# Alternating search depth, and a first search ahead of the projection, in a two-layer graph network kernel

## What is computed

```python
h = relu(layernorm(x))                      # layer 0
src_rows = h[src]                           # 200000 x 32: the gather
msg = sum over 9 coefficients of coef[e,c] * (src_rows @ W0[c])
x = x + segment_sum(msg, dst)

h = relu(layernorm(x))                      # layer 1
msg = sum over 16 bases of wcomp[type[e],b] * (h[src] @ W1[b])
a = tanh(relu(sum((h[src] @ A1.T + b1) * (h[dst] @ A2.T + b2 + rel[type])) / sqrt(32)))
x = x + relu(segment_sum(a * msg, dst) + h[src[last edge]] @ W_self)
```

## Time and profile before

| | us |
|---|---|
| median of 3 runs | 3520.62 (3517.32 to 3525.52) |
| the profiled execution | 3504.08 |
| its span, first to last instruction | 3502.3 |
| PE busy | 3104.4 (89%) |
| DVE busy | 2749.0 (78%) |
| POOL busy | 2353.0 (67%) |
| ACT busy | 883.5 (25%) |

### The profile page before, as it was taken

One profiled execution on the slowest core, in us unless ns is written; L12 is line 12 of the kernel. 1 busy time (PEld: TensorE's weight loads), 2 busy tenths in 40 slices (PEclk: granted clock), 3 DMA queues, 4 the chain that ended last, 5 costly groups with the idle time before them and its releaser, 6 DMA issues. The chain is left out here.

```text
span 3502.3 us, 110849 instructions
## 1 busy us (share of the span) xinstructions
PE 3104.4 (89%) x42844; PEld 2581.4 (74%) x42844; DVE 2749.0 (78%) x4092; ACT 883.5 (25%) x1910; POOL 2353.0 (67%) x2481
## 2 busy tenths in 40 slices
PE   3999999999999999999978888888888888888887
PEld 2777777777777777777767777777777777777776
DVE  7777777777777777777768888888888888888886
ACT  1001001001001001001034443334444444444443
POOL 5666666666666666666537777777777777777772
PEclk9999999999999999999969999999999999999998
DMA  4111111111111111111123333333333333333331
GB/s 130 26 23 25 25 23 25 25 23 25 25 23 25 25 23 25 25 23 25 23 67 57 54 55 56 56 56 56 55 57 57 57 56 56 57 57 56 56 57 39
DMA packets 218214, 149.97 MB, mean 43 GB/s; under 512 B 121914, under 2 KB 199003, under 8 KB 217821
## 3 DMA queue, kind: packets, MB, share of 16 engines
q0 software_dynamic: 79232, 40.73, 11.8%
q1 hardware_dynamic: 138013, 100.79, 11.7%
q10 hardware_dynamic: 576, 2.40, 0.2%
HBM read 135.47 MB, written 8.22 MB: 41 GB/s over the span
## 5 line engine op out<-in xcount | busy, mean ns | idle before, releaser
L538 POOL DMA_INDIRECT xg<-h_table,idx x2476 | 2342.1, 946 | 1091.5 <-issue 721.3
L606 PE MATMUL ps<-h,blocks 128*128 128x448 f32 x9100 | 1921.0, 369 | 23.1 <-DVE blocks L947 23.1
L606 PEld LDWEIGHTS ps<-h,blocks 128*128 128x128 f32 x9100 | 1692.7, 188 | 229.4 <-issue 78.4
L947 DVE TENSOR_TENSOR blocks<-scratch,ps 128x896 fp32r<-128x896 int16 x650 | 703.0, 1082 | 117.1 <-PE ps L606 113.1
L1038 DVE TENSOR_TENSOR Z<-coef,ps 128x864 f32<-128x864 f32 (+1 forms) x522 | 734.3, 1448 | 16.6 <-DVE ps L979 0.2
L672 PE MATMUL ps<-Z,xg 128*32 128x32 f32 (+3 forms) x25008 | 505.9, 215 | 4.9 <-DVE Z L1038 4.9
L826 ACT ACTIVATE p_left<-ps 96x128 f32<-96x128 f32 (+2 forms) x262 | 64.3, 245 | 1734.9 <-PE ps L642 1617.6
L1056 DVE TENSOR_TENSOR aggT<-aggT,ps 64x128 f32 (+1 forms) x262 | 74.1, 283 | 515.0 <-PE ps L654 515.0
L672 PEld LDWEIGHTS ps<-Z,xg 128*32 128x32 f32 x25008 | 403.8, 110 | 88.8 <-issue 67.6
L956 DVE SCALAR_TENSOR_TENSOR scratch<-ramp_sb,scratch,ps 128x448 f32<-128x448 f32 x650 | 438.3, 674 | 0.2
L961 DVE TENSOR_REDUCE xg<-scratch 128x32 f32<-128x448 f32 x650 | 402.7, 620 | 22.3
(11 more groups left out here) (105 smaller groups left out, 1048.7 us busy)
## 6 DMA issues: line engine op xcount, KB each, us to landing
xg<-h_table,idx POOLq DMA_INDIRECT x2476, 2.4
rows_b<-typ_short SPq DMA_DIRECT2D x130, 258.0 KB
scratch<-q_short SPq DMA_DIRECT2D x260, 96.0 KB, 3.3
rows_b<-dst_short SPq DMA_DIRECT2D x130, 126.0 KB
coef<-in_edge_dram SPq DMA_DIRECT2D x130, 54.0 KB, 1.9
att_tab<-p_table SPq DMA_DIRECT2D x393, 8.1 KB
p_table<-Z SPq DMA_DIRECT2D x8, 297.0 KB, 3.8
X<-in_x_dram SPq DMA_DIRECT2D x7, 224.0 KB, 5.0
```

The lines of the kernel that those rows point to most:

```text
L538: pool.indirect_dma_start(xg[:, g.q, t - g.s * J, :], None, h_table[n], bass.IndirectOffsetOnAxis(ap=idx[:, t:t + 1], axis=0)).then_inc(L. ...
L606: last = pe.matmul(found_ps[b], blocks[:, b, c, :], h_2[:, a, c], start=(c == 0 and a == 0), stop=(c == NCH - 1 and a == 1))
L947: dve.tensor_tensor(blocks[:, b], q_b[:, g.b, NPM - NP[n] + i, :].unsqueeze(1).broadcast_to([P, NCH, P]), block_ps.unsqueeze(2).broadcast_ ...
```

## The change

Three things. (1) In layer 0 the number of searched tiles depends on the group: 3 in even groups, 2 in odd ones, where it was 3 in all. POOL gathers the other 9 or 10. Layer 1 keeps 2. (2) In PE's step the search of the group's first tile stands ahead of the projection; the other searches stay behind it. (3) In DVE's step the first mask stands ahead of the addition; `found_rows` makes the addition between the first mask and the first pick. The remaining lines are the counting that goes with it: semaphore values now come from `tiles_before`, buffer parities from the sum of the tiles before, and the loads of the mask numbers always bring three tiles' worth, as before.

```diff
-NP = [3, 2]
-NPM = max(NP)
+NP = [[3, 2, 3, 2], [2, 2, 2, 2]]
+NPM = max(max(np) for np in NP)
...
+    def tiles_before(self, n, later=0):
+
+        r = self.r + later
+        of_pass = FULL // 4 * sum(NP[n]) + sum(NP[n][0:FULL % 4])
+        return self.k * of_pass + (self.i + r // 4) * sum(NP[n]) + sum(NP[n][0:r % 4])
...
-        return [(i, J - NP[n] + i, (self.b * NP[n] + i) % 2, (self.full_order() - 1) * NP[n] + i + 1) for i in range(NP[n])]
+        np = NP[n][self.q]
+        return [(NPM - np + i, J - np + i, (sum(NP[n][0:self.q]) + i) % 2, self.tiles_before(n) + i + 1) for i in range(np)]
...
-                    wait(sp, L.block_set, (g.full_order() - 2) * NP[n])
+                    wait(sp, L.block_set, g.tiles_before(n, -1))
...
                 def step(gs):
+                    tiles = gs[0].found_tiles(n) if gs[0] else []
+                    find_rows(tiles[0:1])
                     if gs[2]:
                         project(gs[2])
-                    if gs[0]:
-                        find_rows(gs[0])
+                    find_rows(tiles[1:])
...
-                def found_rows(new, old):
-
-                    old_tiles = old.found_tiles(n) if old else []
+                def found_rows(new, old, back):
+
+                    old_tiles = old.found_tiles(n)[-2:] if old else []
                     new_tiles = new.found_tiles(n) if new else []
-                    for i in range(max(len(old_tiles), len(new_tiles))):
-                        if new_tiles:
+                    for i in range(max(len(old_tiles), len(new_tiles), 1)):
+                        if i < len(new_tiles):
                             block_rows(new, new_tiles[i])
-                        if i < 2 and old_tiles:
-                            pick_rows(old, old_tiles[i - 2 if NP[n] > 1 else 0])
-                        if i >= 2 and new_tiles:
+                        if i == 0 and back:
+                            add(back)
+                        if i < len(old_tiles):
+                            pick_rows(old, old_tiles[i])
+                        if 2 <= i < len(new_tiles):
                             pick_rows(new, new_tiles[i - 2])
...
                 def step(gs):
-                    if gs[3]:
-                        add(gs[3])
-                    found_rows(gs[0], gs[1])
+                    found_rows(gs[0], gs[1], gs[3])
```

More of the change, by code:

```diff
@@ L86 @@
 assert NOWHERE < 1 << 15 and NREL <= 1 << 8
-assert NCH * MC == M and FULL % 2 == 0 and JT <= JH and PS <= P
+assert NCH * MC == M and FULL % 2 == 0 and all(sum(np) % 2 == 0 for np in NP) and JT <= JH and PS <= P
 def gathers_of_pass(n, q):
-    return len(range(q, FULL, 4)) * (J - NP[n]) + (JT if q == FULL % 4 else 0)
+    return len(range(q, FULL, 4)) * (J - NP[n][q]) + (JT if q == FULL % 4 else 0)
 class Group:
@@ L120, in halves @@
         return -(-self.nj // JH), min(self.nj, JH) * WN
-    def full_order(self):
-        return self.k * FULL + self.s + 1
     def full_order2(self):
@@ L133, in gathers @@
             return gathers_of_pass(n, self.q)
-        return (self.i + self.r // 4 + 1) * (J - NP[n])
+        return (self.i + self.r // 4 + 1) * (J - NP[n][self.q])
     def gathered_tiles(self, n):
-        return self.nj if self.tail else J - NP[n]
+        return self.nj if self.tail else J - NP[n][self.q]
+    def tiles_before(self, n, later=0):
+        r = self.r + later
+        of_pass = FULL // 4 * sum(NP[n]) + sum(NP[n][0:FULL % 4])
+        return self.k * of_pass + (self.i + r // 4) * sum(NP[n]) + sum(NP[n][0:r % 4])
     def found_tiles(self, n):
@@ L597, in edge_sums, with find_rows @@
                 weights = w0c if n == 0 else w1_sb
-                def find_rows(g):
-                    for i, j, b, o in g.found_tiles(n):
+                def find_rows(tiles):
+                    for i, j, b, o in tiles:
                         pe.wait_ge(L.block_set, o)
@@ L663, in sum_edges @@
                     if not g.tail:
-                        pe.wait_ge(L.picked, g.full_order() * NP[n])
+                        pe.wait_ge(L.picked, g.tiles_before(n, 1))
                     pe.wait_ge(L.Z_set, g.order() * 2 - 1)
@@ L946, in block_rows @@
                     wait(dve, L.found, o - 2)
-                    dve.tensor_tensor(blocks[:, b], q_b[:, g.b, NPM - NP[n] + i, :].unsqueeze(1).broadcast_to([P, NCH, P]),
+                    dve.tensor_tensor(blocks[:, b], q_b[:, g.b, i, :].unsqueeze(1).broadcast_to([P, NCH, P]),
                                       block_ps.unsqueeze(2).broadcast_to([P, NCH, P]), ALU.is_equal).then_inc(L.block_set, 1)
@@ L952, in pick_rows @@
                     i, j, b, o = tile
-                    u = g.s * NPM + NPM - NP[n] + i
+                    u = g.s * NPM + i
                     dve.wait_ge(L.found, o)
@@ L1003, in scores @@
                     if not g.tail:
-                        dve.wait_ge(L.picked, g.full_order() * NP[n])
+                        dve.wait_ge(L.picked, g.tiles_before(n, 1))
                     dve.wait_ge(L.ex_done, o)
```

## The result

| | before | the change |
|---|---|---|
| median of 4 runs, us | 3521.82 (3517.32 to 3525.52) | 3295.32 (3294.23 to 3295.84) |
| ratio, 95% interval | 1 | 0.9357 (0.9341 to 0.9373) |
| profiled execution, its span | 3504.08, 3502.3 | 3295.84, 3294.0 |
| last gather, last addition of layer 0 | 1739.95, 1779.99 | 1580.04, 1607.47 |
| first gather, last gather, last addition of layer 1 | 1803.56, 3444.12, 3483.36 | 1630.86, 3258.61, 3275.05 |

The forecast was 3296 us. The time is met, but by luck: two misses cancel in it. From profile to profile the change saves 208.2 us, not 223.6: layer 0 gave 172.5 us where 187.9 were expected, and layer 1, from its first gather to its last addition, 35.6 where 35.7 were.

A forecast was written before the change was run, and what follows sets the result against it. PE was taken to bound layer 0 and POOL layer 1, with POOL next in layer 0; 187.9 + 35.7 = 223.6 us off 3504.1 gives 3280.5, times 1.0047 is 3296 us, range 3283 to 3345.

The forecast's parts named there:

- Depth in layer 0 (189 us of PE): Layer 0: 65 odd groups lose one search of 2.90 us each, 189 us less for PE.
- A gain of about 0.2 us a group, 26 us in all: Layer 0: with the first search ahead of the projection, PE waits about 0.65 us a group instead of 0.85.
- So POOL is the next bound: Layer 0: two groups need 23.7 us of POOL, 22.9 of PE; the layer ends 187.9 us sooner.
- The wait of PE for rows ahead of the sums: Sign expected in layer 0: besides its wait ahead of the first search, PE has another ahead of the sums.
- rival A: PE stays the bound because its new wait exceeds 0.65 us: 150 us gained in all, 3370 us; chance 0.17.
- up to 0.85 us POOL still decides: Layer 0: with PE's new wait up to 0.85 us, POOL, not PE, would still be the bound.
- Layer 1: PE's round falls to 11.8 us, POOL at 12.48 us a group is the bound: 35.7 us less.
- The 0.47%: Whole kernel: the runs' median lay 0.47% above the profiled execution; carried over, 3280.5 us becomes 3296.
- The rule on the shared port: VectorE in a 2-port mode locks GpSimd out; no such instruction is added, so gathers stay at 944 ns.
- B: Layer 1 gains nothing, as DVE becomes its bound through exposed register load and scatter: 3333 us; chance 0.05.
- C: TensorE's clock falls as PE waits for rows before the sums: about 4160 us at a third of both layers; chance 0.03.
- D: The first search is not ahead at all, its pick coming too late: 3335 us as a median; chance 0.05.

The follow-up runs named there:

- e1: Only the alternating depth in layer 0, old order in both layers, against the kernel before on another chip (4876.75 us): costs 2.2%.
- e6: The alternating depth alone in the old order, run again on a further chip where the kernel before takes 4940.36 us; its total is not given, shortest two-search round 10.26 us.
- e4: The kernel before without an edit, profiled on another chip: its one execution took 4869 us, 7 us under the median of the other seven.

## Why the prediction was right, and where it was not

- **Depth in layer 0 (189 us of PE).** Right in kind: 65 searches went to POOL, and a round with two searches is 13.11 - 10.26 = 2.85 us shorter than one with three, where 2.90 were taken as a third of a stretch (the 10.26 is from undisturbed rounds of e1 and e6). 65 x 2.85 is 185 us, more than the whole gain of layer 0.
- **"A gain of about 0.2 us a group, 26 us in all".** This step failed. The wait was 0.77 us, not 0.65: from the end of the pick's multiplication to the search it is 1038.12 - 1037.98 = 0.14 us, not 0.06, and in the even group of the rows shown the pick starts 0.36 us behind the addition, not 0.23. And the border that the projection now makes between searches costs about 0.16 us (8.87 against 8.71, 6.03 against 5.87), which the forecast's value took as nothing and only its upper bound as 0.3. So 0.08 us of waiting was saved and 0.16 spent. Instead of 12.9 and 10.0 us PE needs 13.25 and 10.33. The order costs 0.07 us in an odd group and 0.14 in an even one, 65 x 0.07 + 66 x 0.14 = 14 us in layer 0: 185 - 14 leaves 171, measured 172.5. That the order costs this much is worked out from rounds, those of the depth alone on other chips; no run on the first chip has the depth alone.
- **"So POOL is the next bound".** This fails with it. PE needs 13.25 + 10.33 = 23.58 us per two groups, not 22.9, and POOL's 23.72 is longer by only 0.14. POOL does run without a pause, and its dates were met (fifth group 81.98, forecast 80.7; last gather 1580.04, forecast 1579.6), but its lead was used up only by 12.6 us, the difference of the two tails, instead of 27.5. The wait of PE for rows ahead of the sums, which the forecast named as a sign, isn't there (0.0 us at L675). The layer ended when PE was done, 15.4 us later than forecast. That is rival A in a mild form: the forecast held PE's slack for 27 us, and it was 15 us below zero. By the forecast's own rule, "up to 0.85 us POOL still decides", a wait of 0.77 was harmless; the rule left out the border.
- **Layer 1.** Right, 35.6 against 35.7 us. From first to last gather POOL took 1627.8 us instead of 1640.6, and last gather to last addition shrank by 22.8. The search does start earlier than the projection did: PE waits 102.6 / 113 = 0.91 us where it waited 1.47. But the round fell only from 12.58 to 12.27 us, not to 11.8: here too the searches, 5.78 us in one stretch, take 6.04 in two. PE was nearly the bound again: a group's gathers started 1.7 us behind the release of their buffer at first and 29 at last, and rows were waited for only from 2722 us on, in the last 45 or so groups (37.5 us over 34 waits until 3200 us). The end of the layer is as forecast because POOL never paused and its lead was gone at the end; the slack that the forecast gave PE was not there.
- **Median and profile.** The 0.47% was carried over and is not there. With the profiles' 208.2 us alone the forecast's own way of counting would have said 3311: the 15 us missing in layer 0 and the 0.47% that fell away cancel, and that the forecast hit the time to 1 us is luck. Where the 17 us of the kernel before lie between its runs and its profiled execution is open.
- **The rule on the shared port.** The gathers stay at 944 ns with DVE 72% busy in layer 0 and 88% in layer 1. The Trainium skill, "SBUF — State Buffer", section "SBUF: two separate sides", names a lock by instructions in a 2-port mode, and one by instructions with two SBUF inputs against some of GpSimd's. The trace does not speak against it, as the change adds neither; with DVE's busy shares nearly what they were (73% and 86%) it is no test of denser work.
- **Rivals.** B (layer 1 gains nothing) is refuted by its 35.6 us. C (the clock falls) did not happen where the forecast was made, at 1.00 in both stretches; on the other chips the clock did fall and the change is slower by 1.4%, but there the kernel before has it too, and PE's halts stand ahead of it in the step shown, not waits for rows. D (no gain from the search ahead) holds for layer 0, as the rounds show, where it even costs a little, and not for layer 1.

## What to carry to other kernels

A step moved ahead of a wait meets its own dependency next: work out that one from the timeline, add the border that it makes (look at how long the same work takes in one stretch and in two, as no idle time shows it), and ask whether the buffer behind it can be given away instead. Where a forecast turns on which of two engines is slower by a few per cent, the lead between them decides how much comes out at the end, so count it at both ends of the loop. And a gain measured on one chip need not hold on another: look at the granted clock and the "issue" gaps of the kernel before on each, and when several versions take the same time a group to a tenth of a microsecond, look for what they share.

## What the runs showed of the hardware

The same program took 3522 us on one chip and 4874 to 4940 on three others. There PE stood for 0.2 to 1.2 us (e4, the step shown) between matmuls with nothing to wait for, in layer 1 for 4.5 to 5.5 us a group, and its granted clock was 0.79 to 0.90 on average in the steady stretches with all matmuls, changing between the levels of 2.4 and 1.2 GHz, while POOL's gathers (944 ns) were what they had been. Splitting one stretch of 28 matmuls into two of 14 cost 0.2 us in all (5.87 against 6.07 us), even where neither part waited. A chain of gathers issued by POOL ran at 1.248 us from one to the next on the first chip, 0.944 busy and 0.30 of issue, in both layers.
